# Attention and feed-forward kernel: score matmuls set apart in the up stage, clamps in its first units, eight filler transposes

## What is computed

```python
x = x + xattn(layernorm(x), ctx, ctx, Wq, Wk, Wv, Wfc, bfc)
x = x + ffn(layernorm(x), w_gating, w_linear)

def xattn(q, k, v, ...):      # 32 heads of 16, 8 groups of keys and values, 128 keys
    score = einsum('bhqd,bhkd->bhqk', q @ Wq.T, k @ Wk.T) / 4
    return softmax(score) @ (v @ Wv.T) @ Wfc.T + bfc

def ffn(x, w_gating, w_linear):      # fp8 e4m3 operands, bfloat16 results, hidden 2048
    a = gelu(x @ w_gating[0]) * (x @ w_gating[1])
    return a @ w_linear
```

## Time and profile before

| | |
|---|---|
| median of 3 runs | 447.47 us (446.4 to 447.73) |
| the profiled execution: time / span | 446.08 us / 444.3 us |
| mean granted TensorE clock | 0.996 |
| busy PE / PEld / DVE / ACT / POOL | 422.0 / 328.8 / 333.6 / 309.5 / 237.7 us |
| chain that ended last | PE 78%, DVE 9%, ACT 6%, POOL 3%, issue 3% |
| DMA | 49.66 MB moved, mean 112 GB/s |

### The profile page before, as it was taken

One profiled execution on the slowest core, in us unless ns is written; L12 is line 12 of the kernel. 1 busy time (PEld: TensorE's weight loads), 2 busy tenths in 40 slices (PEclk: granted clock), 3 DMA queues, 4 the chain that ended last, 5 costly groups with the idle time before them and its releaser, 6 DMA issues.

```text
span 444.3 us, 9843 instructions
## 1 busy us (share of the span) xinstructions
PE 422.0 (95%) x3665; PEld 328.8 (74%) x3665; DVE 333.6 (75%) x694; ACT 309.5 (70%) x573; POOL 237.7 (53%) x225
## 2 busy tenths in 40 slices
PE   7897989999999999999999999999999998999997
PEld 6776758787767787778877787778877775578773
DVE  3787789998987789758977789758976785665351
ACT  7748857886797648874797658874797658865450
POOL 5578977994388405971288405971288403940000
PEclk9999999999999999999999999999999999999999
DMA  8867985857415440338015440337013420000001
GB/s 277 312 175 265 346 196 192 221 154 195 145 28 142 97 118 3 83 87 205 11 28 134 110 115 0 81 91 190 25 39 83 108 63 0 27 25 1 0 27 71
DMA packets 21231, 49.66 MB, mean 112 GB/s; under 512 B 4672, under 2 KB 5184, under 8 KB 21184
## 3 DMA queue, kind: packets, MB, share of 16 engines
q1 hardware_dynamic: 20828, 48.22, 38.1%
q10 hardware_dynamic: 356, 0.82, 0.7%
HBM read 23.86 MB, written 4.19 MB: 63 GB/s over the span
## 4 chain that ended last, share of the span: by engine, by line
PE 78%; DVE 9%; ACT 6%; POOL 3%; issue 3%; ACTq 1%; POOLq 0%; DVEq 0%
PE bank L677 24%; PE bank L696 11%; PE bank L464 7%; PE bank L465 7%; PE bank L466 6%; PE bank L551 6%; PE bank L583 5%; PE bank L603 3%; DVE mneg L1125 2%; PE bank L605 2%; POOL plo L1338 2%; PE bank L503 2%; ACT phi L880 2%; PE bank L621 1%; PE bank L517 1%
## 5 line engine op out<-in xcount | busy, mean ns | idle before, releaser
L1338 POOL TENSOR_TENSOR plo<-p,phi 128x512 f16<-128x512 f32 x128 | 152.7, 1207 | 61.6 <-ACT phi L880 60.8
L677 PE MATMUL bank<-x2T,wgate 128*128 128x256 fp8e4 x1024 | 121.7, 273 | 0.0
L677 PEld LDWEIGHTS bank<-x2T,wgate 128*128 128x128 fp8e4 x1024 | 95.9, 98 | 23.0 <-issue 11.6
L1125 DVE TENSOR_REDUCE mneg<-bank 128x4 fp32r<-128x512 f32 x128 | 83.2, 684 | 14.5 <-PE bank L551 12.8
L877 ACT ACTIVATE p<-bank 128x512 f32<-128x512 f32 x128 | 77.7, 607 | 16.7 <-PE bank L583 16.1
L880 ACT ACTIVATE phi<-bank 128x512 f16<-128x512 f32 x128 | 77.5, 606 | 0.0
L902 ACT ACTIVATE gate<-bank 128x512 bf16<-128x512 f32 x64 | 38.2, 597 | 39.1 <-PE bank L677 34.9
L696 PE MATMUL bank<-wlin,act 128*128 128x512 fp8e4 x224 | 64.3, 378 | 0.0
L906 ACT CAST ff<-bank 128x512 bf16<-128x512 f32 x64 | 37.5, 586 | 29.7 <-PE bank L677 29.7
L583 PE MATMUL bank<-qs,ks 98*128 98x512 f32 x128 | 54.4, 425 | 3.6 <-ACT phi L880 2.9
L551 PE MATMUL bank<-kmask,cq 128*128 128x512 f32 x128 | 52.0, 461 | 2.4 <-DVE mneg L1125 1.2
(11 more groups left out here) (121 smaller groups left out, 825.0 us busy)
## 6 DMA issues: line engine op xcount, KB each, us to landing
qs<-cq SPq DMA_DIRECT2D x90, 128.0 KB, 2.4
stage<-in_w SPq DMA_DIRECT2D x14, 512.0 KB, 5.4
ks<-khl SPq DMA_DIRECT2D x96, 64.0 KB, 2.0
cin<-in_ctx SPq DMA_DIRECT2D x8, 512.0 KB, 4.2
xr<-in_x SPq DMA_DIRECT2D x16, 256.0 KB, 3.2
out<-xr SPq DMA_DIRECT2D x16, 256.0 KB, 2.6
xr<-in_w SPq DMA_DIRECT2D x4, 512.0 KB, 5.0
raw_l<-in_w SPq DMA_DIRECT2D x4, 512.0 KB, 5.3
```

The lines of the kernel that those rows point to most:

```text
L677: mm = pe.matmul(out[:, h * TOK:(h + 1) * TOK], wgate8[:, UH * v + h, kk, part, :], x2T[:, pair, kk, :], start=kk == 0, stop=kk == KT - 1)
L1125: dve.tensor_reduce(dst[:, :, 2 * half:2 * half + 2, j].rearrange("p a r -> p r a"), bank_of("S", q, i, s)[:, :].rearrange("p (r a k) -> p ...
L1338: pool.tensor_tensor(plo[:, e % PBUF, :], p32[:, e % P32BUF, :], phi[:, e % PBUF, :], ALU.subtract).then_inc(plo_ok, 1)
```

## The change

The units of the up stage change their order on two engines: on TensorE part 1 of the up projection stands between the two scores of a unit (and ahead of score 5 in unit 2), on VectorE the product and the conversion stand between the two reductions. The clamps of the second up stage go into units 0 to 5. Eight more fillers stand ahead of the transpose of the maxima of pair 1, in bank G1.

```diff
-CLAMPS_UP = ((0, 1, 2), (0, 1, 2, 4, 5, 6))
+CLAMPS_UP = ((0, 1, 2), tuple(range(6)))
@@
-BUSY = dict(max=12, first=2, xn=5, xT=6, early=1, unit=2, row=8)
+BUSY = dict(max=12, first=2, xn=5, xT=6, early=1, max2=8, unit=2, row=8)
@@ turn_max
                     take_bank("M", q, i)
                     keep_busy(m_bank(q, i), BUSY["max"])
+                if q == 1 and i == 0:
+                    keep_busy(G[1], BUSY["max2"])
                 pe.wait_ge(max_ok, TILES * q + SBANKS * (i + 1))
@@ TensorE, up stage
                     for s in score_range(p, k):
+                        if p and s % per == per // 2:
+                            up(p - 1, k, 1)
                         if q < NP and s >= early:
                             scores(q, *divmod(s, SBANKS))
                             if first:
                                 keep_busy(G[1], BUSY["unit"])
-                    if p:
-                        up(p - 1, k, 1)
@@ VectorE, up stage
                     for s in score_range(p, k) if per else ():
+                        if p and s % per == per // 2 and k:
+                            product(u0 + k - 1)
+                            act_fp8(u0 + k - 1)
                         if s >= early:
                             maxima(q, *divmod(s, SBANKS))
-                    if per and p and k:
-                        product(u0 + k - 1)
-                        act_fp8(u0 + k - 1)
```

## The result

The changed kernel takes **443.18 us** (median of 5 runs, 443.01 to 444.28); the kernel before, run beside it, 447.47 us (445.12 to 447.81). The ratio is 0.9934, 95% interval 0.9909 to 0.9959, that is some 2.9 us less. Forecast were 444.4 us and 3.04 us less. (Five executions of the runs told here took 474.75 to 834.06 us, two of the kernel before and one each of e3_order_only, e6_small_clamps and e4_last_fillers, there the profiled one, and are left out of every comparison.)

The account below looks back on a forecast made before the run. TensorE was taken as the bound, dense except in three places. Terms of 0.48 + 2.05 + 0.32 + 0.19 = 3.04 us off the median of 447.47 gave 444.4 us, range 442.8 to 446.5.

Parts of the forecast that it names:

- the three places: Where TensorE is not dense: pair 0's up stage, pair 1's up stage, and the wait for the exponential behind it.
- clock term: Pair 0's up stage: the half-rate stretch goes, and VectorE's three gaps of 0.16 us with it, 0.48 us.
- Eight fillers: Pair 0's up stage: they fit in TensorE's 1.51 us wait, cost nothing and bring 0.48 us, range 0 to 0.9.
- the walk through pair 1's stage: Instruction by instruction: VectorE done 1.2 us earlier, next stage's third score 2.05 us earlier; range 0.4 to 3.55 us.
- Scores apart on TensorE: Up stages: eight up matmuls, one score, twice, take 2.24 us for 2.23, 0.01 us more per unit.
- the credit on the up blocks: Up stages: eight up matmuls before a score take only 0.80 us; without this, switches cost 1.2 us in all.
- Middle stages: Pairs 2 to 5: ScalarE 0.19 us earlier, TensorE 0.13 later, 0.08 us less each, 0.32 in all; pair 7 0.19 less.
- A: Pair 1: only the removed cast pays, TensorE's 2.60 us stay; 1.8 us less in all, 445.7 us, chance 0.2.
- C: Middle stages: VectorE's product and conversion meet GpSimd's subtract, up to 2 us lost in each of four; 452 us, chance 0.07.
- Signs: Clock 1.00 from 64 to 70 us, no VectorE gaps, pair 1's stretch near 15.1 us, middle periods within 0.2 of 49.9.
- signs of being wrong: TensorE waiting for reductions in pairs 2 to 5, lower clock elsewhere, or pair 1's product and conversion over 1.1 us four times.
- a dense stage 1: Pair 1's up stage and the stretch behind it with everything dense: 3.55 us less; the range reached down to half its addition.

Follow-up runs that it names:

- e3_order_only: Kernel before with only the new order on TensorE and VectorE, casts and fillers as before: 445.21 us (nine runs), ratio 0.9974.
- e6_small_clamps: Kernel after with GpSimd's clamps of the second up stage on 16 of 1024 columns, the rest left out: 441.51 us (three runs).
- e4_last_fillers: Kernel after with thirteen more fillers, ahead of the third and fourth score of the last attention stage: 442.6 to 443.2 us in three executions.
- e2_clamps_only: Kernel before with only the clamps of the second up stage moved into units 0 to 5: 446.45 us, ratio 0.9988.
- e1_fillers_only: Kernel before with the eight fillers alone: 446.08 us, ratio 0.9997.
- e5_last_fillers_again: Kernel after with the thirteen fillers in the last attention stage, run a second time: 442.81 us (six runs), ratio to the kernel before 0.9920.
- e8_vector_order_only: Kernel after with TensorE's order put back (both scores together, then the second up block), VectorE's order new: 453.20 us (one run).
- e7_tensor_order_only: Kernel after with VectorE's order put back (both reductions, then product and conversion), TensorE's order new: 450.15 us (one run).

## Why the prediction was right

The time, its sign and nearly its size were right, 3.04 us for the 2.9 measured, and the three places were the right ones. That the size came so close is partly luck. Term by term, in the two profiled executions, the fillers gave 0.71 us for a forecast of 0.48, pair 1 1.45 for 2.05, the later stages 1.03 for 0.51: 3.19 for 3.04, the errors making each other up. At the same mean clock the change is worth some 2.1 us, where the forecast without its clock term has 2.56.

*Eight fillers, 0.48 us.* The mechanism holds: they fit in the wait, the stretch at half rate in pair 0's stage goes, VectorE's gaps with it. Mis-sized: the stage shrinks by 0.71 us, since VectorE lost more than the three gaps I counted: from the first of its eight reductions to its next work took 5.91 us before (64.01 to 69.92) and 5.08 after (63.78 to 68.86). And the term counts only in an execution in which the clock falls there. The upper steps of the kernel before are more runs of that kind than I could see in three. The Trainium skill, "TensorE: Matmul & The Clock Gate", section "HAM oscillation — how this bites in real kernels", puts such falls down to long waits of TensorE between bursts, and by it this term was nothing. The runs decide otherwise. In the three profiles with the wait of 1.51 us (before, e2_clamps_only, e3_order_only) the clock falls in the wait or within 1.8 us of its end; in the four of e1_fillers_only, after, e5_last_fillers_again and e6_small_clamps, where the fillers leave 0.64 or 0.65 us, it is 1.00 from 64 to 68.5 us.

*Clamps, with the walk through pair 1's stage, 2.05 us.* Measured 1.45. The cast's part is 0.95 us alone. The step that failed is the walk: "conversion 3 to 113.1" behind a free product 3. A product and a clamp that start 0.02 us apart decide up to 0.9 us (1.30 us for the 0.41 of a free one), and my walk had not that precision. It isn't a toss of a coin, though: the meeting repeats in three traces. The conversion before it ends 0.27 us behind GpSimd's second clamp (108.06 + 1.14 against 107.71 + 1.22), and from there each engine has some 1.1 us to go, two reductions here, what is left of a subtract there. VectorE's end of the stage came 0.33 us earlier by the stage's own clock, not 1.2. The range given for this term, 0.4 to 3.55 us, held it.

*Scores apart on TensorE, 0.01 us a unit.* Right: 0.80 and 0.32 us. The upper end of this term was added up wrongly: both scores of a unit become lone ones, 0.09 us a unit without the credit on the up blocks, so 2.7 us in 30 units and not 1.2. It didn't matter, as the credit is real.

*Middle stages, 0.08 us each and 0.19 in the last, 0.51 in all.* Measured 1.03 us, about 0.2 in each. ScalarE's earlier exponential was right: it begins 0.20 us earlier in the stage (15.55 us behind the first up block, before 15.75), and TensorE's wait of about 0.2 us for it is gone. What I missed is at the joint: the last score now stands directly ahead of the next stage's first, and first to second-in-line falls from 0.31 us (220.11 to 220.42, with fp8 ahead of the first) to 0.23 (217.61 to 217.84). I had charged the first score's 0.13 us later and not this 0.08 us back.

*Rivals.* A, that the cast alone pays in pair 1, is nearer to the truth there than my forecast: 0.95 of 1.45 us. C, VectorE late in the middle stages, didn't come: products behind the subtract last 0.77 and 0.67 us and not 1.3 us, and TensorE waits for no reduction. With TensorE's order alone VectorE does meet the subtracts, and a period takes 50.7 us.

*My baseline.* I put the 1.4 us between the profiled execution and the median of three down to nothing in particular. It fits the second fall of the clock, in the last attention stage, which the change doesn't touch; no profile of the kernel before caught it, but that of e3_order_only, at the same 0.992, shows both falls.

*Signs.* The clock, the missing gaps, the normalization under 0.8 us, the missing cast and wait and the starts of 0.80 and 0.32 us came as said. The stretch of pair 1 (15.84 us for 15.1) didn't, and the middle periods, 49.62 to 49.68 us, are a little better than the 49.7 I allowed. One of my signs of being wrong came out: the lower clock stands elsewhere in the profiled execution. The change didn't bring it there, going by the 0.992 step of the kernel before; but I had not seen that the place existed. As to the range, 442.8 us takes in all of the 1.5 us that a dense stage 1 would add, not half of it as the text says.

## What to carry to other kernels

Where a time comes in steps, sort the executions by their mean granted clock before you compare medians: here a part worth 0.95 us on the path moved the median not at all, and with fillers in the second place, found only so, the slow step was gone. Interleave on both engines of a producer and its consumer, or on neither: one alone cost 6 to 9 us here. And a walk through two engines that block each other is good for the sum of the work, not for which meetings happen; give such a term its whole range.

## What was not expected of the hardware

The lower clock followed the same wait in some executions and not in others. Behind TensorE's 1.48 us wait of the earlier trace rows the clock stayed at 1.00 in the profiles of before, e1_fillers_only and e2_clamps_only and fell to 0.50 in that of e8_vector_order_only; behind the 1.23 us wait in the same place it fell in those of after, e3_order_only and e7_tensor_order_only and stayed at 1.00 in that of e6_small_clamps. The kernel with the fillers alone splits five to five. The cost is steady: from the third score of p = 7 to the end take 71.1 to 71.2 us in the five profiles without this fall and 72.7 us in the four with it, 1.5 us; between the steps of the run times it is 1.1 to 1.5 us. One in pair 0's stage costs 0.7 us of the stage and some 0.9 us between the steps (446.1 against 445.2).
